# Turning an expert's gathered rows with a DMA transpose from ScalarE's queue instead of TensorE transposes

## What is computed

```python
x = x + _L0_xattn_ref(_layernorm(x), ctx_1024, mask, Wq, Wk, Wv, Wo)     # x: (16, 256, 512)
x = x + _L0_ffn_ref(_layernorm(x), gate_w, gate_bias, w1, w2, w3, shared_gate, shared_up, shared_down)
...
def _moe(x, topk_idx, topk_w, w1, w2, w3):        # 4096 tokens, 32 experts, 4 chosen, 128 slots an expert
    buf = jnp.zeros((E, CAP, H), x.dtype).at[flat_e, slot].set(x_rep, mode='drop')
    h = silu(einsum('ech,ehf->ecf', buf, w1)) * einsum('ech,ehf->ecf', buf, w3)   # H=512, F=256
    ob = einsum('ecf,efh->ech', h, w2)
...
shared = silu(x @ shared_gate) * (x @ shared_up) @ shared_down     # for every token
```

## Time and profile before

| | |
|---|---|
| median of 3 runs | 1640.73 us (1638.84 to 1643.18) |
| profiled execution | 1646.64 us, of which 1644.9 us are the span |
| PE busy | 1605.2 us (98% of the span) |
| DVE, ACT, POOL busy | 1215.0, 844.8, 793.6 us |
| granted TensorE clock, mean | 0.994 |
| DMA packets | 399662, 218.28 MB |

### The profile page before, as it was taken

How to read it: one execution, slowest core, us unless ns; L and a number is a source line. 1 busy time by engine, 2 the same in 40 slices (tenths; PEclk the granted TensorE clock), 3 DMA queues, 4 the chain that set the end, 5 groups by cost and what they waited for, 6 DMA issues and landing times. The chain is left out here.

```text
span 1644.9 us, 35029 instructions
## 1 busy us (share of the span) xinstructions
PE 1605.2 (98%) x12199; PEld 1147.0 (70%) x12199; DVE 1215.0 (74%) x3524; ACT 844.8 (51%) x2094; POOL 793.6 (48%) x1088
## 2 busy tenths in 40 slices
PE   8999999999999999999999999999999999999995
PEld 5667677777777777777777677777777666666663
DVE  7988787777778787787778787877766266776762
ACT  6764444454454454454545454454433266666662
POOL 3443646455564646464554646464345423433422
PEclk9999999999999999999999999999999999999998
DMA  8765444364555445445445444544476578988834
GB/s 261 179 155 110 105 97 111 73 116 79 116 98 115 112 85 110 91 111 97 118 98 111 103 104 105 97 104 91 92 243 199 112 237 225 265 238 219 232 40 55
DMA packets 399662, 218.28 MB, mean 133 GB/s; under 512 B 348400, under 2 KB 356592, under 8 KB 399488
## 3 DMA queue, kind: packets, MB, share of 16 engines
q1 hardware_dynamic: 383024, 189.71, 46.6%
q0 software_dynamic: 15904, 25.29, 9.2%
q10 hardware_dynamic: 560, 1.05, 0.2%
HBM read 91.87 MB, written 40.80 MB: 81 GB/s over the span
## 5 line engine op out<-in xcount | busy, mean ns | idle before, releaser
L957 ACT ACTIVATE arena<-arena,neg_max 128x256 f32<-128x256 f32 x512 | 253.7, 496 | 377.9 <-DVE neg_max L1260 306.2
L704 POOL TENSOR_SCALAR arena<-arena,prob_scale 128x256 f16<-128x256 f32 x384 | 184.4, 497 | 474.9 <-DVE prob_scale L1269 451.7
L1629 PE MATMUL ps_query<-xn_both,arena 128*128 128x256 f16 x1024 | 279.1, 273 | 0.7 <-DMA xn_both<-xn_half 0.7
L1631 PE MATMUL ps_query<-xn_both,arena 128*128 128x256 f16 x1024 | 279.1, 273 | 0.0
L1630 PE MATMUL ps_query<-xn_both,arena 128*128 128x256 f16 x1024 | 279.1, 273 | 0.0
L1260 DVE CUSTOM_DVE_ANT_0 arena<-ps_score,mask_add 128x256 f32<-128x256 f32 x512 | 186.2, 419 | 78.2 <-PE ps_score L1631 78.2
L1275 DVE SCALAR_TENSOR_TENSOR arena<-arena,prob_scale 128x256 f16<-128x256 f32 x384 | 236.8, 665 | 6.1 <-POOL arena L704 6.1
L1629 PE MATMUL ps_out<-arena,o_t 128*128 128x512 f16 x512 | 194.2, 379 | 1.8 <-DVE o_t L1280 1.7
L1630 PE MATMUL ps_out<-arena,o_t 128*128 128x512 f16 x512 | 194.0, 379 | 0.0
L1631 PE MATMUL ps_out<-arena,o_t 128*128 128x512 f16 x512 | 194.0, 379 | 0.0
L1280 DVE SCALAR_TENSOR_TENSOR o_t<-ps_head,o_t 128x512 f16<-128x512 f32 x128 | 88.3, 690 | 108.6 <-ACT o_t L970 107.8
(11 more groups left out here) (337 smaller groups left out, 4063.0 us busy)
## 6 DMA issues: line engine op xcount, KB each, us to landing
arena<-w SPq DMA_DIRECT2D x96, 512.0 KB, 6.0
out_rows_dram<-weight_in POOLq DMA_DIRECT2D x32, 256.0 KB, 4.8
x_in<-x SPq DMA_DIRECT2D x15, 512.0 KB, 3.9
out_rows_dram<-x SPq DMA_DIRECT2D x30, 256.0 KB, 2.4
xn_rows<-xn_half SPq DMA_DIRECT2D x15, 512.0 KB
x2t_kept<-xn_both SPq DMA_DIRECT2D x12, 512.0 KB, 2.9
ctx_in<-ctx_t SPq DMA_DIRECT2D x16, 256.0 KB, 3.0
weight_in<-wq SPq DMA_DIRECT2D x8, 512.0 KB, 5.3
```

The source lines that it names most:

```text
L704: pool.tensor_scalar(p_rows[:, c, 0, :], probs[:, c, :], prob_scale[:, c:c + 1], 1.0, ALU.mult, ALU.mult).then_inc(norm_hi, 1)
L957: act.activation(probs[:, c, :], probs[:, c, :], ACT.Exp, bias=neg_max[:, c:c + 1], scale=-1.0, accum_out=prob_sum[:, c:c + 1]).then_inc(e ...
L1629: pe.matmul(dst, a.hi, b.hi, start=start and n == 0, stop=False)
L1631: m = pe.matmul(dst, a.lo, b.hi, start=False, stop=stop and n == len(pairs) - 1)
```

## The change

Four things change together.

1. expert_rows and copy_rows are gone. In the place of copy_rows, ACT issues a DMA transpose (turn_rows) of the whole gathered tile, 128 rows by 1024 float16, straight into the SBUF tile that expert_up reads. It waits for the gather and for expert_up of two experts before.
2. expert_up on PE waits for that transpose, and gather on POOL waits for it before it overwrites a rows buffer. There are two semaphores, for even and odd experts.
3. A DMA transpose keeps blocks of 128 neighbouring features. So x1_norm writes the normalized row in the order in which w1 and w3 lie: it reads x1 with a step of four floats (16 bytes), four blocks of 128, and writes contiguously. The number of instructions is the same.
4. The gate and the shared gate and up weights, which multiply the same rows, are loaded with four (two per load) neighbouring rows to a partition.

```diff
-                    pool.tensor_scalar(xn2_full[:, t, :], x1[:, t, :], mean_var[1][:, t, 0:1], rstd[1][:, t:t + 1],
+                    pool.tensor_scalar(by_blocks(xn2_full[:, t, :]), by_turned_rows(x1[:, t, :]), mean_var[1][:, t, 0:1], rstd[1][:, t:t + 1],
                                        ALU.subtract, ALU.mult).then_inc(x1_normed, 1)
...
             def gather(e):
                 if e >= ROWS:
-                    pool.wait_ge(pe_rows, e - ROWS + 1)
+                    pool.wait_ge(rows_turned[(e - ROWS) % 2], 16 * ((e - ROWS) // 2 + 1))
...
-            def copy_rows(e):
-                act.wait_ge(pe_rows, e + 1)
+            def turn_rows(e):
+                act.wait_ge(gathered[e % ROWS], 16 * (e // ROWS + 1))
                 if e >= 2:
                     act.wait_ge(pe_eup, e - 1)
-                act.activation(rows_both[e % 2], ps_rows.rearrange("p (h k c) -> p h k c", h=2, k=KD), ACT.Copy,
-                               scale=1.0).then_inc(rows_copied, 1)
+                act.dma_start_transpose(rows_both[e % 2].rearrange("p h k c -> p (h k) c"), rows_in[e % ROWS]).then_inc(
+                    rows_turned[e % 2], 16)
...
-            def expert_rows(e):
-                pe.wait_ge(gathered[e % ROWS], 16 * (e // ROWS + 1))
-                if e:
-                    pe.wait_ge(rows_copied, e)
-                else:
-                    pe.wait_ge(placed, B)
-                rows = rows_in[e % ROWS].rearrange("c (h p k) -> c h k p", h=2, k=KD)
-                for n in range(2 * KD):
-                    m = pe.transpose(ps_rows[:, n * P:(n + 1) * P], rows[:, n // KD, n % KD, :], ident_half)
-                m.then_inc(pe_rows, 1)
-
             def expert_up(e):
-                pe.wait_ge(rows_copied, e + 1)
+                pe.wait_ge(rows_turned[e % 2], 16 * (e // 2 + 1))
...
                 if 1 <= e <= E:
                     expert_down(e - 1)
-                if e + 2 < E:
-                    expert_rows(e + 2)
                 if e < E:
                     expert_hidden(e)
```

More of the change, by code:

```diff
@@ L272, in build @@
         ps_last = [ps[:, :].bitcast(F16) for ps in ps_score]
-        ps_rows = ps_fill[1][:, :].bitcast(F16)
         def piece_bank(k):
@@ L304, in build @@
             signal(n) for n in ("pe_x2t", "pe_gate", "pe_rank", "pe_up", "pe_down"))
-        pe_rows, pe_eup, pe_eht, pe_ey = (signal(n) for n in ("pe_rows", "pe_eup", "pe_eht", "pe_ey"))
+        pe_eup, pe_eht, pe_ey = (signal(n) for n in ("pe_eup", "pe_eht", "pe_ey"))
         weight_hi, xn_hi, key_hi, query_hi, value_hi, head_hi, xn2_hi, ctx_hi, norm_hi = (
@@ L324, in build @@
             signal(n) for n in ("gate_exp", "used", "weighed", "placed", "slotted"))
-        ident_halved, last_copied, rows_copied = (signal(n) for n in ("ident_halved", "last_copied", "rows_copied"))
+        ident_halved, last_copied = signal("ident_halved"), signal("last_copied")
+        rows_turned = [signal(f"rows_turned{n}") for n in range(2)]
         tanhed, hid, staged = (signal(n) for n in ("tanhed", "hid", "staged"))
@@ L335, in rows_of, with turned_rows_of, by_blocks, by_turned_rows @@
             return w.rearrange("(k p) n -> p k n", p=P)
+        def turned_rows_of(w):
+            return w.rearrange("(p k) n -> p k n", p=P)
+        def by_blocks(row):
+            return row.rearrange("p (k q) -> p k q", k=KD)
+        def by_turned_rows(row):
+            return row.rearrange("p (q k) -> p k q", k=KD)
         def by_columns(name, dst, src, rows, n, width, buf):
@@ L341, in by_columns, with by_rows @@
             return (name, n), dst[:, :, at], rows_of(src)[:, :, at], rows, width, buf
-        def by_rows(name, dst, src, rows, cols, n, buf):
+        def by_rows(name, dst, src, rows, cols, n, buf, of=rows_of):
             at = slice(n * rows, (n + 1) * rows)
-            return (name, n), dst[:, at, :], rows_of(src)[:, at, :], rows, cols, buf
+            return (name, n), dst[:, at, :], of(src)[:, at, :], rows, cols, buf
         jobs = [by_columns("wk", wk_s, wk, KC, 0, 512, 0), by_columns("wq", wq_s, wq, KD, 0, 256, 1),
@@ L355, in build @@
             jobs.append(by_rows("wo", wo_s, wo, PAIR, D, c, len(jobs) % 4))
-        jobs += [("gate", gate_s, rows_of(gate_t), KD, E, 0)]
-        jobs += [by_rows("sg", sg_s, shared_gate, 2, FS, n, (1, 2)[n]) for n in range(2)]
-        jobs += [by_rows("su", su_s, shared_up, 2, FS, n, (3, 0)[n]) for n in range(2)]
+        jobs += [("gate", gate_s, turned_rows_of(gate_t), KD, E, 0)]
+        jobs += [by_rows("sg", sg_s, shared_gate, 2, FS, n, (1, 2)[n], turned_rows_of) for n in range(2)]
+        jobs += [by_rows("su", su_s, shared_up, 2, FS, n, (3, 0)[n], turned_rows_of) for n in range(2)]
         jobs += [by_rows("sd", sd_s, shared_down, 2, D, n, (2, 3)[n]) for n in range(2)]
@@ L1090, in act_program @@
                 piece(k)
-            copy_rows(0)
+            for e in range(2):
+                turn_rows(e)
             piece(EARLY - 1)
-            copy_rows(1)
             for e in range(E + 2):
@@ L1111, in act_program @@
                 if e + 2 < E:
-                    copy_rows(e + 2)
+                    turn_rows(e + 2)
                 if HELD <= e + 2 < E:
@@ L1173, in x1_norm @@
                 for t in range(TB):
-                    dve.tensor_scalar(xn2_full[:, t, :], x1[:, t, :], mean_var[1][:, t, 0:1], rstd[1][:, t:t + 1],
+                    dve.tensor_scalar(by_blocks(xn2_full[:, t, :]), by_turned_rows(x1[:, t, :]), mean_var[1][:, t, 0:1], rstd[1][:, t:t + 1],
                                       ALU.subtract, ALU.mult).then_inc(x1_normed, 1)
@@ L1881, in pe_program @@
             rank(ps_fill[1], z)
-            for k in range(11, EARLY - 1):
+            for k in range(11, EARLY):
                 piece(k)
-            expert_rows(0)
-            piece(EARLY - 1)
-            expert_rows(1)
             for e in range(E + 2):
```

## The result

The changed kernel takes **1703.36 us** (median of 4 runs, 1697.85 to 1710.05) against 1639.78 us of the kernel before on the same chip (1637.57 to 1643.18): ratio 1.0388, 95% interval 1.0343 to 1.0432. The profiled execution took 1701.03 us; its span is 1699.3 us, 54.4 us over the 1644.9 of before. In what follows a ratio leaves out executions over 1.5% longer than the fastest of the same kernel (two with unread transposes from ACT, one each of the layout half, which took 6862 us, of the run with more lead and of the run with swapped roles), while a median keeps them.

A forecast was written before the change was run, and what follows sets the result against it. PE, busy throughout the expert stage, was taken as the bound: -14.1 (removed transposes) + 0.7 (first entry) + 0.4 (iteration 0) = -13.0 us, which from the runs' median of 1640.73 gives 1628 us, range 1624 to 1640.

The forecast's parts named there:

- one transpose occupies the 16 engines for 1.5 us: Expert stage, DMA engines: price of a transpose, taken from the attention stretch; 21 transposes add 31 us.
- the 12 us of backlog fall on the weight stream: Expert stage: 213 us of DMA work in 201 leave 12 us, covered by 48 us of weight lead, costing nothing.
- Landing in the loop: Expert loop: each transpose is issued 1.5 iterations (15 us) ahead of its use and lands within 2.8 to 5.7 us.
- if expert_up waits for xn_both in the loop: Expert loop on PE: a listed sign that the forecast is wrong, expert_up waiting for its transposed rows; no size given.
- The issue on ACT: Expert loop on ACT: most of a transpose's 1.27 us issue hides under an activation, leaving a gap of about 0.3 us.
- the DMA engines become the bound: Rival, expert stage: a transpose takes 4 us of the engines, giving 1645 us; decides from 3.8 us on; chance 0.06.
- PE's price of 0.44 us a group: Expert stage on PE: removing 32 groups of eight transposes, 0.44 us each, gains 14.1 us.
- The entry: First expert_up on PE: it waits 0.7 us for the first transpose, 3.3 us with a landing of 5.7 us.
- iteration 0: PE's second piece in the first expert iteration: 0.44 us given back as wait, about 1.1 us of wait in all.
- The layout: x1_norm on POOL, attention stage: the 16-byte step costs 0.3 us an instruction, hidden, since up to 0.70 us is free.
- the two rivals on x1_norm: Strided x1_norm read on POOL: read half as much again, 1638 us, chance 0.06; x1_norm doubled, 1669 us, chance 0.06.
- The wait on POOL: POOL's gathers wait 3 to 6 us for a transpose's landing, twice per six experts, without delaying the path.

The follow-up runs named there:

- unread transposes from ACT: Kernel before with five weight buffers, plus 32 DMA transposes of a constant tile, issued by ACT, into tiles nobody reads: 1708.21 us, ratio 1.0314.
- the layout half: Kernel before with only the strided x1_norm and the regrouped gate and shared weight loads; TensorE still turns the rows: 1643.93 us, ratio 1.0005.
- the run with more lead: Changed kernel with transposes issued four experts ahead instead of two, into six tiles, with five weight buffers: 1693.74 us, ratio 1.0312.
- the run with swapped roles: Kernel before, five weight buffers, weight loads of experts 5 to 31 from ACT, 32 unread transposes from SP: 1688.05 us; control without transposes 1636.56 us.
- unread twins: Kernel before, five weight buffers, plus 32 transposes nobody reads: issued by ACT 1708.21 us, ratio 1.0314; issued by SP 1639.77 us, ratio 1.0007.
- light loads: Weight loads of experts 6 to 31 cut to an eighth: changed kernel 1624.32 us, ratio 0.9896; kernel before 1636.26 us, ratio 0.9980.

## Why the prediction was wrong

The forecast was 1628 us with a range of 1624 to 1640; 1703 came.

**The step that failed** is the one on the DMA load: "one transpose occupies the 16 engines for 1.5 us", and from it "the 12 us of backlog fall on the weight stream" at no cost. The 1.5 us came from the attention stretch, where the transposes stand in the one queue that also carries the plain loads, and where the engines are half filled (0.50). That price nearly holds in one queue (2.1 us beside the weight stream, at about 4 us of time in all). It does not hold for transposes from a second queue: 4.3 us for one and 2.1 us more for the loads beside it. The slowing was shown by the unread twins (ACT 1.031, SP 1.001) and by the swapped roles. What in the engines makes two queues slow, no run tells. The cost did not fall where the prediction put it, on the weights' lead: that held. It fell on the landings, on the gathers and on ACT.

**Landing in the loop.** 15 us of lead against 3.1 to 5.7 us of landing was taken as safe; the landings were 11.7 us in the median and up to 30.6. This is the wait that PE shows, but not a cause by itself: with four experts of lead it vanished and 51 us of loss stayed. The prediction had named "if expert_up waits for xn_both in the loop" as a sign of being wrong, and it came. (The landings in the earlier trace rows are of all DMAs into xn_both; those of L512 alone are 3.0, 3.2 and 5.1 us.)

**The issue on ACT.** "Bounds: 0 and the full 1.27 us" was too narrow: up to 7.67 us, and 59.3 us of hold in the run with more lead. The bound was from the attention stage and its half-filled engines. Two queues are not needed for this: with all in SP's queue an issue held SP up to 7.2 us, at no harm, since SP computes nothing.

**The rivals.** The nearest was named, "the DMA engines become the bound", with its deciding point at 3.8 us; the measured 6.4 us by its own formula give 21 x 6.4 - 67 = 67 us late, less 13.0: 1695. That this is near the result is in part luck: the formula has the weights late once their lead is used up, and no weight load was waited for; also 6.4 us of packets overlap with others. Its chance of 0.06 was too low: the one price it was held against, 1.5 us, was from another setting of queues, although the 86.7% of filled engines had been read. The Trainium skill (Advanced Engine Details and Errata, "X-Bar Transpose (TRN2)") rates a transposing DMA as fast as a regular one; the plain copy of the same packets took 1.2 us of the engines, the transpose 2.1 in the loads' queue and 4.3 in another, so the measurement differs.

The one wait of this kind at the entry, in the changed kernel:

```profile
1296.14 0.39 PE L1638 MATMUL ps_score<-arena,xn_both 128*128 128x512 f16 x1 [0.86 <-DMA xn_both<-x_in]
```

**What was right.** PE's price of 0.44 us a group: 13.8 us measured with light loads (give or take 4) against a sum of 13.0. The entry, 0.86 us of wait against 0.7, and iteration 0, 1.2 us with light loads against 1.1. The layout costs nothing: 0.51 us against 0.3 forecast and 0.70 free; the two rivals on x1_norm fell. The Trainium skill (GPSIMD Engine Reference, "Performance pitfalls for Q7 kernels") gives half as much again for a read with such a step, by which the instruction would take 1.08 us more, an estimate; the row says 0.51. The wait on POOL was rightly placed; its size, 3 to 6 us, was off with the landing (57.7 us in five waits).

## What to carry to other kernels

Price a DMA transpose in the company it will have: which queue issues it, what another queue carries meanwhile, and how full the engines are; a duration from a stretch with one queue says little for two. Put transposes that run beside a load stream into that stream's queue, with enough tiles and lead that 12 us of landing are covered, and keep them off a compute engine's queue. A moved wait is not a removed cost: before deepening a buffer, run the transfers with nobody waiting for them.

## What was not expected of the hardware

- Transposes and loads from two queues: 39.89 MB (changed kernel) and 38.51 MB (unread) moved in 210 us of filled engines, against 54.02 and 56.96 MB from one.
- A plain copy with the same 1024 packets costs the engines 1.2 us and no time that shows.
- The issue of a transpose holds the engine that issues it up to 7.67 us in the changed kernel and SP up to 24.0 us in the run with swapped roles (1.23 to 1.25 us at the least). The issue of a plain weight load beside transposes of the other queue took 0.33 us in the median and 0.86 at most in the swapped run, but up to 5.22 us (median 0.36) on SP in the changed kernel.
- In one queue a transpose lands after 11.7 us in the median among the loads and is harmless when it is issued early enough; one expert later the same transposes cost 37 us.
